# Layer 0 of a two-layer transformer kernel: bias passes off TensorE's order, expert sums in the scores' bank, value products one step later

## The reference

```python
qkv = einsum('bnm,fm->bnf', x, Wqkv).reshape(b, n, 16, 24)
q, k, v = qkv[..., :8], qkv[..., 8:16], qkv[..., 16:]
scores = einsum('bnhd,bngd->bnhg', q, k) / 8
out = einsum('bnhg,bngd->bnhd', softmax(scores), v)
x = layernorm(x + out.reshape(b, n, 128) @ Wproj.T + bproj)
logits = x @ gate_w.T + gate_b            # 8 experts, the top 2 kept
gate_score = softmax(logits of the top 2, the others -inf)
expert_out = einsum('bsd,edo->bseo', x, expert_w) + expert_b
x = layernorm(x + einsum('bseo,bse->bso', expert_out, gate_score))
```

## Time and profile before

| | |
|---|---|
| median of 3 runs | 2282.39 us (2275.52 to 2288.68) |
| the profiled execution | 2284.86 us, its span 2283.1 |
| granted TensorE clock, mean of the span | 0.965 |
| PE / DVE / ACT / POOL busy, whole span | 93% / 78% / 69% / 48% |

### The profile page before, as it was taken

How to read it: one execution, slowest core, us unless ns; L and a number is a source line. 1 busy time by engine, 2 the same in 40 slices (tenths; PEclk the granted TensorE clock), 3 DMA queues, 4 the chain that set the end, 5 groups by cost and what they waited for, 6 DMA issues and landing times. The chain is left out here.

```text
span 2283.1 us, 61127 instructions
## 1 busy us (share of the span) xinstructions
PE 2112.3 (93%) x16512; PEld 1592.5 (70%) x16512; DVE 1788.3 (78%) x5918; ACT 1567.1 (69%) x3951; POOL 1099.1 (48%) x2407
## 2 busy tenths in 40 slices
PE   5999999999699999999999999999999993999990
PEld 3777777777467677667766766776676672999990
DVE  6788888887078888888888888888888885677775
ACT  2555555555378787788787878878787882777774
POOL 4667667676122434444443444444344435344444
PEclk9999999998799999999999999999999996999995
DMA  1000000000100000000000000000100000222226
GB/s 34 20 25 21 21 28 21 23 25 14 56 1 2 11 2 11 11 6 7 11 11 2 11 11 8 5 11 11 77 10 11 9 4 30 60 66 65 64 62 221
DMA packets 63497, 62.92 MB, mean 28 GB/s; under 512 B 9691, under 2 KB 58471, under 8 KB 62713
## 3 DMA queue, kind: packets, MB, share of 16 engines
q1 hardware_dynamic: 54764, 42.64, 6.2%
q0 software_dynamic: 8448, 16.93, 2.3%
HBM read 33.17 MB, written 22.69 MB: 24 GB/s over the span
## 5 line engine op out<-in xcount | busy, mean ns | idle before, releaser
L1359 DVE SCALAR_TENSOR_TENSOR restT<-ps_t,leadT 128x512 f16<-128x512 f32 (+1 forms) x768 | 459.3, 598 | 136.8 <-ACT leadT L1286 105.8
L1286 ACT ACTIVATE leadT<-ps_t 128x512 f16<-128x512 f32 (+1 forms) x768 | 403.0, 525 | 138.3 <-PE ps_t L1152 137.5
L1135 PE MATMUL ps_s<-xT_all,qm 128*128 128x512 f32 (+1 forms) x1024 | 489.8, 560 | 0.8 <-ACT qm L1267 0.8
L1152 PEld LDWEIGHTS ps_t<-ident,p 128*128 128x128 f32 x2560 | 315.9, 141 | 232.9 <-issue 169.5
L1152 PE MATMUL ps_t<-ident,p 128*128 128x128 f32 x2560 | 413.2, 276 | 8.2 <-DVE restT L1359 6.4
L1277 ACT ACTIVATE p<-ps_s,neg_max 128x512 f32<-128x512 f32 (+1 forms) x512 | 326.1, 637 | 77.1 <-DVE neg_max L1349 64.5
L1349 DVE CUSTOM_DVE_ANT_0 ps_s<-ps_s,mask 128x512 f32<-128x512 f32 (+1 forms) x512 | 319.9, 625 | 43.0 <-PE ps_s L1135 42.8
L979 POOL CAST v_parts<-v_all 128x36 bf16<-128x36 f32 x256 | 57.3, 224 | 560.4 <-PE ps_o L1166 560.2
L1135 PEld LDWEIGHTS ps_low<-xT_all,qm 128*128 128x128 f32 x1024 | 194.6, 190 | 135.5 <-issue 122.3
L1126 PE MATMUL ps_qm<-xT_all,m_head 128*128 128x512 f32 x512 | 264.2, 598 | 0.3 <-issue 0.3
L261 POOL TENSOR_TENSOR pv_prod<-probs,kv 128x2048 f32<-128x2048 f32 x64 | 259.5, 4076 | 0.1
(11 more groups left out here) (223 smaller groups left out, 4336.6 us busy)
## 6 DMA issues: line engine op xcount, KB each, us to landing
row_in<-rows_dram SPq DMA_DIRECT2D x136, 65.0 KB
y<-results SPq DMA_DIRECT2D x16, 512.0 KB, 5.2
xT<-in_xT SPq DMA_DIRECT2D x32, 128.0 KB, 2.1
xres<-in_xT SPq DMA_DIRECT2D x32, 128.0 KB, 2.1
xT_all<-x2T SPq DMA_DIRECT2D x32, 128.0 KB, 2.0
out_x<-x SPq DMA_DIRECT2D x16, 256.0 KB, 3.2
xT_all<-in_wide SPq DMA_DIRECT2D x1, 2760.0 KB
results<-row_out,row_in POOLq DMA_INDIRECT x136
```

Source lines behind the costliest of these rows:

```text
L1135: mm = pe.matmul(ps_s[n], qm[j][:, n * P:(n + 1) * P], xT_all[:, bass.ds(b * S, (n + 1) * P)], start=True, stop=True)
L1152: mm = pe.transpose(ps_t[g][:, at + n * P:at + (n + 1) * P], probs[i][:, n * P:(n + 1) * P], ident[:, :])
L1286: act.activation(leadT[j][g][:, :], ps_t[g][:, 0:width[g]], ACT.Copy, scale=RAISE)\
L1359: dve.scalar_tensor_tensor(out=restT[j][g][:, :], in0=ps_t[g][:, 0:width[g]], scalar=RAISE, in1=leadT[j][g][:, :], op0=ALU.mult, op1=ALU.s ...
```

## The change

- `bproj` is a column now, and POOL adds it to the residual `xres` (`bias_residual`, new, L304, last in POOL's step) before PE's `project` reads it; the four bias passes of `project` go. PE waits for the new semaphore `xres_biased` in place of the load.
- `logits` lays one bias pass pair over both tiles' columns (`gateb_sb` holds the bias twice) instead of one for each tile. `sum_experts` lays the expert biases of both tiles in one pass pair of 256 columns.
- `ps_r2T` moves from `ps_tail` to `ps_scores` (the bank that DVE's `qk_sums` writes). PE's `sum_experts` waits until the scores of the pair three later are shifted, and DVE's `qk_sums` waits for `copy_r2T`. `ps_v` moves from `ps_tail` to `ps_turn`, where `ps_oT` is; `sum_heads` waits for `copy_v`.
- The pipeline has a sixth part. `values` and `copy_v` run one step later (`part[5]`), PE's right after `sum_experts`, ACT's after `copy_x1T`; layer 0 has one step more at its end.
- PE: `turn_gates` moves ahead of `turn_x2` and `project`, and waits for `copy_oT`. ACT: `copy_gT` and the last `apply_gates` move ahead of `copy_x2T` and `exponentials`. POOL: `inverse1` moves ahead of `normalise`. DVE's order stays.

```diff
-            for s in range(NP - 1, NP + 3):
+            for s in range(NP - 1, NP + 4):
...
-        ps_r2T, ps_r2 = ps_tail[:, 2 * P:4 * P], ps_tail[:, 0:2 * P]
-        ps_x2T, ps_v = ps_tail[:, 2 * P:4 * P], ps_tail[:, 0:2 * P]
+        ps_r2T, ps_v = ps_scores[:, 0:2 * P], ps_turn[:, 0:2 * P]
+        ps_x2T, ps_r2 = ps_tail[:, 2 * P:4 * P], ps_tail[:, 0:2 * P]
...
+                def bias_residual(u, j):
+                    s = 2 * u + j
+                    pool.wait_ge(xres_loaded[j], 16 * (u + 1))
+                    pool.sem_inc(pool_passed, 1)
+                    pool.tensor_tensor(xres[j][:, :], xres[j][:, :], bproj_sb[:, :].to_broadcast([P, 2 * P]), ALU.add)\
+                        .then_inc(xres_biased, 1)
...
                 def step(u, j, part):
-                    if part[2]:
-                        normalise(*before(u, j, 1))
                     if part[3]:
                         inverse1(*before(u, j, 2))
                     if part[2]:
+                        normalise(*before(u, j, 1))
                         pv_products(*before(u, j, 1), 0)
                         pv_products(*before(u, j, 1), 1)
                     if part[4]:
                         inverse2(*before(u, j, 3))
+                    if part[1]:
+                        bias_residual(u, j)
...
                     if a == 0:
                         when(pe, oT_sb, s)
                         when(pe, x1T_sb, s)
+                        when(pe, v_sb, 2 * (s - 2))
...
-                    pe.wait_ge(xres_loaded[j], 16 * (u + 1))
+                    pe.wait_ge(xres_biased, s + 1)
...
-                        pe.matmul(tile(ps_r1, a), tile(attnT, a), wproj_sb[:, :], start=True, stop=False)
-                        pe.matmul(tile(ps_r1, a), ones[0:1, 0:P], bproj_sb[:, :], start=False, stop=False)
-                        mm = pe.matmul(tile(ps_r1, a), tile(xres[j], a), ident[:, :], start=False, stop=True,
+                        pe.matmul(tile(ps_r1, a), tile(attnT, a), wproj_sb[:, :], start=(a == 0), stop=False)
+                    for a in range(2):
+                        mm = pe.matmul(tile(ps_r1, a), tile(xres[j], a), ident[:, :], start=False, stop=(a == 1),
                                        is_transpose=True)
...
-                    for a in range(2):
-                        pe.matmul(tile(ps_logits, a, E), tile(x1T, a), gatew_sb[:, :], start=True, stop=False)
-                        mm = pe.matmul(tile(ps_logits, a, E), ones[0:1, 0:P], gateb_sb[:, :], start=False, stop=True)
+                    pe.matmul(ps_logits, ones[0:1, 0:P], gateb_sb[:, :], start=True, stop=False)
+                    for a in range(2):
+                        mm = pe.matmul(tile(ps_logits, a, E), tile(x1T, a), gatew_sb[:, :], start=False, stop=(a == 1))
...
                     pe.wait_ge(gates_ready, s + 1)
+                    pe.wait_ge(oT_sb, min(s + 2, NP) if isinstance(s, int) else s + 2)
...
-                    when(pe, v_sb, 2 * s)
-                    for a in range(2):
-                        pe.matmul(tile(ps_r2T, a), expb_sb[:, :], tile(gatesT, a), start=True, stop=False)
+                    pe.wait_ge(scores_shifted, 2 * min(s + 3, NP) if isinstance(s, int) else 2 * (s + 3))
+                    pe.matmul(ps_r2T, expb_sb[:, :], gatesT[:, :], start=True, stop=False)
+                    for a in range(2):
...
@@ ACT's step @@
                     if part[2]:
                         copy_oT(*before(u, j, 1))
+                    if part[3]:
+                        copy_gT(*before(u, j, 2))
+                        apply_gates(*before(u, j, 2), 1, 1)
                     if part[4]:
                         copy_x2T(*before(u, j, 3))
                     if part[1]:
                         exponentials(u, j)
-                    if part[3]:
-                        apply_gates(*before(u, j, 2), 1, 1)
-                        copy_gT(*before(u, j, 2))
-                    if part[4]:
-                        copy_v(*before(u, j, 3))
...
                     when(dve, scores_shifted, 2 * s)
+                    when(dve, r2T_sb, s - 2)
```

More of the change, by code:

```diff
@@ L86, in layer0 @@
         wproj_sb = sb("wproj_sb", [P, P])
-        bproj_sb = sb("bproj_sb", [1, P])
+        bproj_sb = sb("bproj_sb", [P, 1])
         gatew_sb = sb("gatew_sb", [P, E])
-        gateb_sb = sb("gateb_sb", [1, E])
+        gateb_sb = sb("gateb_sb", [1, 2 * E])
         expw_sb = sb("expw_sb", [P, E * P])
@@ L147, in layer0 @@
         xres_loaded = [sem(f"xres_loaded{j}") for j in range(2)]
+        xres_biased = sem("xres_biased")
         x2T_kept = [sem(f"x2T_kept{j}") for j in range(2)]
@@ L175, in one @@
             def one(s):
-                step(s // 2, s % 2, tuple(0 <= s + 1 - n < NP for n in range(5)))
+                step(s // 2, s % 2, tuple(0 <= s + 1 - n < NP for n in range(6)))
             for s in range(5):
@@ L179, in steps @@
             with eng.Fori(2, NP // 2 - 1) as u:
-                step(u, 1, (True,) * 5)
-                step(u + 1, 0, (True,) * 5)
-            for s in range(NP - 1, NP + 3):
+                step(u, 1, (True,) * 6)
+                step(u + 1, 0, (True,) * 6)
+            for s in range(NP - 1, NP + 4):
                 one(s)
@@ L308, in step @@
                         inverse2(*before(u, j, 3))
+                    if part[1]:
+                        bias_residual(u, j)
+                pool.wait_ge(weights_in, 16 * NWEIGHTS)
                 steps(pool, step)
@@ L391, in sum_experts @@
                             mm = pe.matmul(tile(ps_r2T, a), tile(gated[a], e), ident[:, :], start=False,
-                                           stop=(e == E - 1), is_transpose=True)
+                                           stop=(a == 1 and e == E - 1), is_transpose=True)
                         mm.then_inc(r2T_ps, 1)
@@ L418, in step @@
                         sum_experts(*before(u, j, 3))
+                    if part[5]:
+                        values(*before(u, j, 4))
                     if part[3]:
@@ L438, in step @@
                         four_experts(*before(u, j, 2), 1, 1)
+                        turn_gates(*before(u, j, 2))
                     if part[4]:
@@ L442, in step @@
                         project(*before(u, j, 1))
-                    if part[3]:
-                        turn_gates(*before(u, j, 2))
-                    if part[4]:
-                        values(*before(u, j, 3))
                 qkv_products(0, 0, 0)
@@ L547, in step @@
                         copy_x1T(*before(u, j, 2))
+                    if part[5]:
+                        copy_v(*before(u, j, 4))
+                    if part[3]:
                         gate_exp(*before(u, j, 2))
@@ L1972, in laid_out @@
         "wproj": i["L0_attn_Wproj"].T,
-        "bproj": i["L0_attn_bproj"].reshape(1, P),
+        "bproj": i["L0_attn_bproj"].reshape(P, 1),
         "gate_w": i["L0_ffn_gate_w"].T,
-        "gate_b": i["L0_ffn_gate_b"].reshape(1, E),
+        "gate_b": np.stack([i["L0_ffn_gate_b"]] * 2).reshape(1, 2 * E),
         "expert_w": i["L0_ffn_expert_w"].transpose(1, 0, 2).reshape(P, E * P),
```

3 lines of the change are left out of this document (1 added, 2 removed).

## The result

| | before | changed |
|---|---|---|
| median of the runs | 2279.88 us (4 runs, 2275.52 to 2288.68) | 2359.10 us (4 runs, 2357.75 to 2360.41) |
| ratio, 95% interval | | **1.0342** [1.0309, 1.0376] |
| span of the profiled execution | 2283.1 us | 2358.7 us |
| mean granted clock, whole span | 0.965 | 0.932 |

What follows compares the result with a forecast made beforehand. PE was taken to bound the kernel before, with DVE near; after the change, a loop through ACT's exponentials. 2284.9 + 24 (longer loop) + 45 (PE's clock falling) = 2354 us, range 2306 to 2376.

Steps and rivals of the forecast that it cites:

- The chain: Layer 0's loop from DVE's moments through POOL, PE and ACT's exponentials back: 17.9 us a step against 17.06, +24 us.
- the walk: Link-by-link sum of profiled times from DVE's L588 to the next L588 in layer 0, ending at 17.9 us.
- PE idles before turn_x1, and the clock falls in most steps: In layer 0 PE idles 2.2 to 2.3 us awaiting normalised x1; its clock falls, 1.6 us a step, +45 us.
- My 1.9: Clock price, in us, of a layer 0 step whose logits, four_experts and qkv all lose full rate on PE.
- the discount for steps that keep the clock: Clock price taken as 1.6 us instead of 1.9, as some layer 0 steps regain the clock sooner or keep it.
- Filling and draining, counted as nothing: Start and end of layer 0's pipeline: a few us either way, none counted.
- PE's saving: Layer 0 step on PE: project 0.7, logits 0.3, expert sums 0.3, value-copy wait 0.7; together 2.0 us.
- POOL's addition of the bias: Last in POOL's step: 0.5 us, hidden, ending near 13.3 while project wants it at 14.6.
- What the profile should show: Layer 0: exponentials' wait 2.3 to 2.6 us, reciprocals 19 to 20 apart, PE about 85% busy, clock 0.8 to 0.9.
- The rule on short idle times: Skill page's claim that short idle times between PE's matmul groups make the clock swing; it favoured the forecast with falls.
- the chain with the clock held: Rival: layer 0's longer loop alone, PE's clock not falling, 2309 us; chance 0.20.
- The faster case: Rival: exponentials don't hold DVE in layer 0, step 15.6 us, -41 us, 2244 us; chance 0.04.

Runs made afterwards that it cites:

- doubling one link: Changed kernel with three unread 512-column products on PE before turn_x1, plus the last four gated experts computed again on ACT ahead of the exponentials; ratio 1.0310.
- moves alone: Kernel before, with turn_gates early on PE, gate copy and last gated experts ahead of ACT's exponentials, inverse1 ahead of normalise on POOL; ratio 1.0279.
- bias parts alone: Kernel before, with only the bias added on POOL and the logits' and experts' bias passes merged; orders, banks and stages as before; ratio 0.9956.
- values first: Changed kernel with ACT's exponentials ahead of the gates' work, POOL's normalise ahead of inverse1, and PE's values ahead of sum_experts; ratio 0.9863.
- three products thrown away: Changed kernel with three extra 512-column products, results unread, on PE between values and turn_x1; ratio 1.0126.
- exponentials first: Changed kernel with ACT's exponentials right behind copy_oT, ahead of gate copy, last gated experts and x2T copy; ratio 0.9823.
- those with two: Changed kernel with two extra 512-column products, results unread, on PE between values and turn_x1, alone (1.0137) or with POOL's normalise first (1.0033).

## Why the prediction was right

- *The chain* (17.9 us, +0.84 a step, +24 us): right. Held at full clock it is 18.04, +0.98 a step, 27 us. Each station of the walk was met to within 0.1 us, doubling one link added its price, and removing the block of ACT's work that closes the loop took 4.1 us off a step. The walk's links add up to 17.83, rounded up to 17.9; the steps measured are 17.70 and 18.41 in turn, and the walk knew nothing of that difference (below).
- *PE idles before turn_x1, and the clock falls in most steps* (2.2 to 2.3 us; 1.6 us a step, +45): the mechanism was right, the size too small. PE idles 2.3 to 2.9 us, and the clock costs 2.13 us a step, 60 us. My 1.9 for a step that loses logits, four_experts and qkv was nearer, and the discount for steps that keep the clock was not due: four_experts took 3.3 to 3.8 us in every step of the stretch. That the idle time is what makes the clock fall is shown only so far: work in its place brings the clock back. The moves alone lost it in 13 steps with waits of at most 0.8 us, so an idle time of 2 us is not needed for it.
- *Filling and draining, counted as nothing*: wrong by -12.4 us, 10.6 of it in the drain. About half of that is the clock of the kernel before, by an estimate from its trace: in its drain the expert sums, four_experts and the first sum_heads of a step took 14.71 us (558.11 to 572.82, most of it at 1.2 GHz), where the same groups at full clock take 8.71 (5.14 from 579.75, 1.82 and 1.75 from 547.51). The changed kernel lost the clock there only for one four_experts (3.30 us instead of 1.96). The rest is not assigned. 28 x 3.11 = 87 us less 12.4 gives 74.6, where the forecast had 69. Two mis-sized terms, clock and drain, of opposite sign, made the total better than its parts. That closeness was luck: with nothing for the drain these steps would have given 2372, near the end of the range.
- *PE's saving* (1.3 us without the wait): somewhat low, in the changed kernel 1.7. Project, from L353 to L396, takes 0.76 us (318.89 to 319.65) where it took 1.79, so 1.0 rather than 0.7; the logits 0.78 in the kernel with the bias parts alone (297.42 to 298.20) instead of 1.26 in the kernel before (308.17 to 309.43); the expert biases 0.62 (319.65 to 320.27) instead of 0.8, so 0.2. As forecast, it brought nothing in the changed kernel, since PE isn't what bounds it.
- *POOL's addition of the bias*: 0.61 us, where I had 0.5 from normalise's row. By the add in the page "GPSIMD Engine Reference" of the Trainium skill (section "Performance versus the Vector engine") it would be 0.56, an estimate. Hidden, as stated: it ends at 315.24, and project comes at 318.9.
- *What the profile should show*: clock 0.84, PE busy 86%, no wait for v_all: as said. The reciprocals stand 20.1 to 20.7 us apart in most steps, where 19 to 20 was forecast: the clock's cost again. The value products start 2.5 us after inverse1, not 2.3. Wrong was the exponentials' wait, 4.7 us in place of 2.3 to 2.6. The lower figure holds for the chain alone (2.42 with the clock held); I left out that whatever the clock costs also ends in this wait.
- *The rule on short idle times* ("TensorE: Matmul & The Clock Gate", section "A second HAM failure mode: psum-queue depth-cycling" of the Trainium skill): the traces agree that short idle times can be enough. They don't agree with each other on how long: with one idle time of 0.7 us a step the clock held in 27 of 28 (the kernel before), but with waits of at most 0.8 it fell in 13 (the moves alone); at 1.33 and 1.50 in turn it fell in most (the bias parts alone), but at 0.99 and 1.44 in turn it held in 22 (values first); at 2.3 to 2.9 it fell in every step. So the length of the idle time doesn't decide it alone, and what else does was not tried.

The upper end of the range, 2376, doesn't follow from the 2.3 us of clock that it names; with those it would be 2373. Nothing hangs on it.

The rivals: the chain with the clock held is the kernel with three products thrown away, 1.0126, where 2309 / 2284.9 = 1.0105 was forecast. The faster case needed ACT's exponentials not to hold DVE; "exponentials first" takes that hold away and is faster, 0.9823.

## What to carry to other kernels

Before an operation is moved ahead of another on an in-order engine, walk the loop that closes through it, from rows: here ACT was 56% busy and still had no room in that one place, and the 2 us a step that PE saved were worth nothing. Look at what idle time a changed stream of matmuls leaves, and where: the clock's fall cost twice what the longer chain did. Where PE waits anyway, a product thrown away is a quick test of whether the clock is what is paid for.

## What the runs showed of the hardware that was not expected

- Less work on PE can lower its clock. With the bias passes gone and nothing else changed, the granted clock in layer 0 fell from 0.99 to 0.92 and took most of the gain; one product of 512 columns in the idle time, read by nobody, brought it to 1.00 and the ratio from 0.9956 to 0.9823. Whether the longer idle time alone does it, or also the missing passes before it, was not separated.
- Moving work can lower it as well, with all passes kept and no idle time of PE over 0.8 us in the 28 steps: the moves alone ran at a granted clock of 0.93.
- With the chain as the only bound every second step is 0.71 us longer, 17.70 and 18.41, alike in the kernel with three products thrown away and, where the clock held, in those with two and with the moves alone. The loop body holds two steps, and in the longer ones DVE stands 0.37 us that the profile ascribes to no engine, right behind the reciprocal (row 313.43), where the earlier trace rows has 0.38; POOL's walk is 0.12 us longer too. That the loop's branch on each engine is the cause fits the place and wasn't tried. In the kernel before, where PE bounds, the steps alternate by 0.1 only.
